# Splitting the column one-hot instruction of an edge placement in two, in a graph network and mixture-of-experts kernel

## The reference

```python
x = x + gnn(layernorm(x), W1, b1, W2, b2, edges=(src, dst))
#   agg  = segment_sum(x[dst], src);  mean = agg / max(count, 1)
#   gnn  = x @ W1.T + b1 + mean @ W2.T + b2
x = x + moe(layernorm(x), Wg, bg, w1, b1, w2, b2)
#   top 2 of 8 experts by score, softmax over the two scores,
#   each expert: relu(x @ w1[e].T + b1[e]) @ w2[e].T + b2[e]
```

## Time and profile before

| | |
|---|---|
| median of 3 runs | 1958.64 us (1956.25 to 1959.66) |
| span of the profiled execution, first to last instruction | 1953.6 us |
| runs' median less that span | 5.0 us |
| PE, PEld, DVE, ACT, POOL busy, share of the span | 90, 76, 50, 57, 61% |
| granted TensorE clock, mean over the span | 0.981 |

### The profile page before, as it was taken

How to read it: one execution, slowest core, us unless ns; L and a number is a source line. 1 busy time by engine, 2 the same in 40 slices (tenths; PEclk the granted TensorE clock), 3 DMA queues, 4 the chain that set the end, 5 groups by cost and what they waited for, 6 DMA issues and landing times.

```text
span 1953.6 us, 41490 instructions
## 1 busy us (share of the span) xinstructions
PE 1762.7 (90%) x11167; PEld 1488.9 (76%) x11167; DVE 967.4 (50%) x2315; ACT 1118.8 (57%) x3316; POOL 1194.5 (61%) x1141
## 2 busy tenths in 40 slices
PE   6888998899887888878887889999999999999997
PEld 4655875588555677656665768999999999999997
DVE  6868977898467887633334786311111111111111
ACT  5964875477544699765652667544444444444443
POOL 1167777778777777777777753454454455444543
PEclk9989999999999999999999999999999999999999
DMA  9323333333333333344543777724424424242421
GB/s 313 102 87 103 94 97 103 103 88 87 100 103 106 100 97 96 100 128 138 143 138 110 236 243 242 216 40 124 127 44 117 102 60 123 38 126 38 124 36 20
DMA packets 113112, 224.31 MB, mean 115 GB/s; under 512 B 27286, under 2 KB 76604, under 8 KB 107094
## 3 DMA queue, kind: packets, MB, share of 16 engines
q0 software_dynamic: 61152, 129.45, 26.6%
q1 hardware_dynamic: 32576, 74.98, 11.3%
q10 hardware_dynamic: 19254, 18.32, 3.0%
HBM read 371.77 MB, written 34.91 MB: 208 GB/s over the span
## 4 chain that ended last, share of the span: by engine, by line
PE 45%; POOL 30%; issue 11%; DMA 6%; DVE 4%; ACT 1%; SPq 1%; DVEq 0%; POOLq 0%; ACTq 0%
POOL arena L650 30%; PE bank L1315 19%; PE bank L1331 18%; DMA arena<-ytab,arena 4%; PE bank L1280 2%; PE bank L1055 2%; PE bank L1303 1%; PE bank L1101 1%; DVE agg L1949 1%; DMA gw<-in_gw2t 1%; SPq L465 1%; DMA ytab<-arena 1%; DMA agg<-in_b 0%; ACT arena L738 0%; ACT arena L753 0%
## 5 line engine op out<-in xcount | busy, mean ns | idle before, releaser
L650 POOL DMA_INDIRECT arena<-ytab,arena x784 | 801.5, 1022 | 240.1 <-issue 228.9
L1280 PE MATMUL bank<-arena 128*128 x2356 | 627.5, 393 | 121.3 <-SPq L525 120.5
L1280 PEld LDWEIGHTS bank<-arena 128*128 128x128 f32 x2356 | 412.4, 195 | 221.4 <-issue 160.7
L948 ACT ACTIVATE arena<-bank,agg 128x128 f32<-128x128 f32 x840 | 308.7, 368 | 400.4 <-PE bank L1315 343.0
L1315 PEld LDWEIGHTS bank<-arena,agg 128*128 128x128 f32 x3360 | 392.2, 192 | 5.6 <-issue 0.7
L1315 PE MATMUL bank<-arena,agg 128*128 128x128 f32 x3360 | 393.8, 276 | 0.3 <-issue 0.3
L1949 DVE TENSOR_TENSOR agg<-agg,bank 128x257 f32 x589 | 247.8, 421 | 292.8 <-PE bank L1280 252.7
L1331 PE MATMUL bank<-agg,arena 128*128 128x256 f32 x1680 | 380.1, 379 | 0.3 <-DMA agg<-in_b 0.3
L683 POOL DMA_INDIRECT out<-arena x105 | 171.0, 1629 | 323.6 <-issue 229.3
L1331 PEld LDWEIGHTS bank<-agg,arena 128*128 128x128 f32 x1680 | 311.0, 190 | 38.5 <-DMA agg<-in_b 0.6
L794 ACT ACTIVATE arena<-lanes,arena 128x128 f16<-128x128 f16 x816 | 247.9, 386 | 21.2 <-DVEq L1577 21.2
(11 more groups left out here) (275 smaller groups left out, 1655.3 us busy)
## 6 DMA issues: line engine op xcount, KB each, us to landing
agg<-in_w SPq DMA_DIRECT2D x210, 1024.0 KB
agg<-in_b SPq DMA_DIRECT2D x105, 128.0 KB
arena<-ytab,arena POOLq DMA_INDIRECT x784
ytab<-arena SPq DMA_DIRECT2D x12, 512.0 KB, 3.2
arena<-in_xt ACTq DMA_DIRECT2D x24, 256.0 KB, 2.9
node<-in_x SPq DMA_DIRECT2D x6, 896.0 KB, 12.3
agg<-in_xt SPq DMA_DIRECT2D x6, 896.0 KB, 12.9
out<-node ACTq DMA_DIRECT2D x6, 896.0 KB
```

What stands on the lines that cost most here:

```text
L650: pool.indirect_dma_start(out=rows[:, v % RU, h, 0:D], out_offset=None, in_=ytab[:, :], in_offset=bass.IndirectOffsetOnAxis(ap=rowidx[g % ...
L948: act.activation(hT[:, m, :], hidden_bank(j, m)[:, 0:T], ACT.Relu, bias=b1b[:, b, m:m + 1]).then_inc(s_fr, 1)
L1280: mm = pe.matmul(bank[bank_of(n)][:, 0:W], onehot[n // QUAD % 2][:, n % QUAD, h, :], pair[:, h * W:(h + 1) * W], start=(h == 0), stop=(h = ...
```

## The change

From the second group on (s = 1, 2, 3) the one instruction that makes the column one-hot of a tile is made as two, for the first four edge columns and for the last four. The second carries the semaphore increment. Both write the same buffer as before, with the same values. For s = 0 the instruction stays whole. Number of tiles that it touches: 22 + 30 + 32 = 84.

```diff
--- before.py
+++ after.py
@@ -1470,8 +1470,14 @@
                 if j % PB == 2:
                     v.wait_ge(s_ohf, OH0[s + 1])
                 v.tensor_tensor(in_pairs(ohq[j % PB][0:EP]), counted(PC, P), pairs(pos_cq[0:EP, 1, c:c + PC, :], PC, P), ALU.is_equal).then_inc(s_q, 1)
-                v.tensor_tensor(in_pairs(ohc[j % PB][0:EP, :, 0:CH[s]]), counted(PC, CH[s]), pairs(pos_cq[0:EP, 0, c:c + PC, :], PC, CH[s]),
-                                ALU.is_equal).then_inc(s_c, 1)
+                if s:
+                    h = PC // 2
+                    v.tensor_tensor(in_pairs(ohc[j % PB][0:EP, 0:h, 0:CH[s]]), counted(h, CH[s]), pairs(pos_cq[0:EP, 0, c:c + h, :], h, CH[s]), ALU.is_equal)
+                    v.tensor_tensor(in_pairs(ohc[j % PB][0:EP, h:PC, 0:CH[s]]), counted(h, CH[s]), pairs(pos_cq[0:EP, 0, c + h:c + PC, :], h, CH[s]),
+                                    ALU.is_equal).then_inc(s_c, 1)
+                else:
+                    v.tensor_tensor(in_pairs(ohc[j % PB][0:EP, :, 0:CH[s]]), counted(PC, CH[s]), pairs(pos_cq[0:EP, 0, c:c + PC, :], PC, CH[s]),
+                                    ALU.is_equal).then_inc(s_c, 1)
                 v.wait_ge(s_q, j + 1)
                 if s == 0:
                     m = PC - BY_ACT
```

## The result

The changed kernel takes 1945.49 us (median of 4 runs, 1942.63 to 1947.36), beside 1959.15 us for the kernel before (4 runs, 1956.25 to 1961.55). The ratio is 0.9934 with a 95% interval of 0.9919 to 0.9950, so the change takes off 13 us, between 10 and 16. Forecast were 1945.6 us and a gain of 13 us.

What follows compares the result with a forecast made beforehand. The prediction took POOL's back-to-back gathers, stretched by DVE instructions, to bound the kernel. From the median of 1958.6 us it took 13 us, the middle of 15.0 and 10.8, giving 1945.6 us, range 1939 to 1953 us.

Steps and rivals of the forecast that it cites:

- POOL sets the pace and the end follows it: The 784 gathers on POOL never wait for the ring; a saving before 1106.85 us moves all that follows.
- A two-input DVE instruction holds a gather until 0.13 us before its end: A gather starting while L1473 runs is held; 45 such gathers were stretched by 27.2 us in all.
- The second half lets the gather in: A waiting gather goes on between L1473's halves; the rival, shut out by the second, meant 1963.3 us, chance 0.05.
- Durations and price on DVE: Halves of L1473 take 0.510, 0.643 and 0.672 us; 84 extra instructions cost 5.9 us of DVE time, hidden beside the gathers.
- The gain, 31.4 - 16.4 or 27.2 - 16.4, middle 13 us: Gather stretch saved on L1473: 15.0 us by rule on both sides, 10.8 us from the observed stretch; 13 us taken.
- if it meets an instruction at a random moment: Stretch rule for gathers every 1.25 us: mean w x w / (2 x 1.25 us) per instruction, w = duration - 0.13 us.
- Nothing else changes: Beyond L1473's hold nothing moves: the semaphore comes 0.07 us later in a tile, and no DMA is added.
- The 5.0 us that the prediction put outside the span: The runs' median lay 5.0 us above the profiled span of 1953.6 us, and was taken as unchanged.
- the phases don't mix: Rival: gathers let go sooner meet the next DVE instruction, giving back 4 us or double; 1952 us, chance 0.07.
- The signs: Expected in the trace: gathers' busy sum about 788 us, last start near 1135 us, stretch falling most beside group 2's placement.
- Held by one instruction only: A stretched gather waits for the end of the DVE instruction it starts in, not for the next one.
- The next list: Rival: group 1's row numbers, ready 6.3 us early, come too late for POOL; half the gain lost, 1952 us, chance 0.07.

Runs made afterwards that it cites:

- 50 whole: Kernel before plus 50 unused two-input DVE instructions of 125 x 2000 f16 beside group 3's gathers; 1984.05 us, ratio 1.0112.
- 50 pairs: Kernel before plus, at 50 places beside group 3's gathers, two unused two-input DVE instructions of 125 x 1000 f16 each; 1972.42 us, ratio 1.0062.
- 50 with one input: Kernel before plus 50 unused DVE reductions over 1024 f16 elements, one SBUF input, beside group 3's gathers; 1961.51 us, ratio 0.9999.
- tiny: Kernel before, L1473 whole, with one 125 x 1 DVE instruction put in front of it in each of the 84 tiles; 1960.43 us, ratio 1.0002.
- the three with 50 additions: Kernel before with 50 whole, 50 pairs or 50 with one input added beside group 3's gathers; 1984.05, 1972.42 and 1961.51 us.
- Six and two: Kernel before with the column one-hot of groups 1 to 3 cut into six edge columns, then two; 1953.37 us, ratio 0.9968.
- quarters: Kernel before with the column one-hot of groups 1 to 3 in four instructions of two edge columns each; 1935.78 us, ratio 0.9878.
- the uneven cuts: Kernel before with the column one-hot of groups 1 to 3 in two uneven pieces, in either order; 1953.37 and 1944.91 us.
- quarters, wide: As quarters, with L1405 also in two and L1661 in two (f16) or four (f32); 1933.52 us, ratio 0.9878 to the kernel before.
- others: Kernel before, L1473 whole, with L1472 and L1486 of groups 1 to 3 each made in two; 1958.06 us, ratio 0.9997.
- tile halves: Changed kernel with L1472 and L1486 of groups 1 to 3 in two as well; 1947.45 us, ratio 0.9939 to the kernel before.
- eighths: Kernel before with the column one-hot of groups 1 to 3 in eight instructions, one per edge column; 1982.96 us, ratio 1.0116.
- all split: As tile halves, with L1405 of groups 1 to 3 in two and L1661 in two (f16) or four (f32); 1939.09 us, ratio 0.9894.
- two and six: Kernel before with the column one-hot of groups 1 to 3 cut into two edge columns, then six; 1944.91 us, ratio 0.9933.

## Why the prediction was right, point by point

- **POOL sets the pace and the end follows it.** Right. Fourteen kernels with the last gather from 1122.6 to 1177.6 us end 805 to 810 us later.
- **A two-input DVE instruction holds a gather until 0.13 us before its end.** Right, and shown apart: 22.3 us for 50 whole, 11.2 us for 50 pairs, 1.1 us for 50 with one input.
- **The second half lets the gather in.** Right for halves, where it was given 0.05 against. It fails for most gathers that start in pieces of 172 to 250 elements, and now and then for others: twice in tiny, with L1473 whole.
- **Durations and price on DVE.** L1475 and L1476 take 0.51, 0.64 and 0.67 us as forecast (0.68 in one group). The price of the instruction is hidden; tiny showed it.
- **The gain, 31.4 - 16.4 or 27.2 - 16.4, middle 13 us.** The net was met, 12.9 us by the ratio, but out of two errors that cancel, so that the number is in part luck. First, 27.2 instead of 31.4 is habit and not chance: the four other kernels that keep L1473 whole and in its place (the three with 50 additions, and tiny) have 30.7, 27.5, 27.6 and 26.3 us of hold by it. Secondly, the halves hold for 8.6 us, not 16.4. So L1473's part of the gain is 27.2 - 8.6 = 18.6 us, over the 15.0 that the sum had as its upper end. The term that failed is "if it meets an instruction at a random moment". L1473 stands behind L1472. A start that falls into L1472 is moved to that one's end, and the next comes 1.25 us after it, beyond the pair. Only starts in the first 0.65 us behind L1472 are free to happen. With the same lengths w that gives 27.7 us whole and 10.8 us halved. The starts bear it out: in the kernel before and the three with 50 additions, 186 gathers start within a whole L1473, all in its first 0.61 us, although it lasts up to 1.2 us. In tiny, 46 start in the first 0.60 us and 16 at 1.14 to 1.15 us, where the hold is over. Six and two bear it out in who is hit, not in how much time the order costs.
- **Nothing else changes.** Wrong by some 5 us, the 18.6 less the 12.9. A gather let go sooner starts its successor sooner, and what ends at L1486 (now L1492) rose from 5.2 to 7.8 us, at L1661 from 8.9 to 10.1 us. How much each takes is not shown by one trace: in the five kernels with L1473 whole in its place L1486 has 4.6 to 9.2 us, in quarters 7.6, and in the uneven cuts 10.7 and 12.7. L1405 rose from 2.8 to 6.1 us, but in the four kernels with L1473 whole it has 6.1, 4.6, 7.8 and 5.0 us, so there the kernel before's own trace was low. That is also why the two profiles differ by 10.4 us in the gathers' busy time and the medians by more. The 5.0 us that the prediction put outside the span were too many: the changed kernel's profiled execution took 1946.23 us at a span of 1944.1, 2.1 us outside. The profiled execution of before was thus near 1955.7 us, below its fastest timed run, and the gain had to be taken from the medians, as it was. This is the rival "the phases don't mix" in a small measure; it ate 5 us, not 8.
- **The signs.** The busy sum came to 791.1 us where about 788 were named, and the last gather starts 2.4 us later than the 1135 named. Stretch was to fall most beside group 2's placement, but fell by 3.5 us there and beside group 1's, and by 7.1 us beside group 3's.
- **Held by one instruction only.** Not so for all gathers of the kernel before: its longest, 2.41 us from 136.11 us on, and one of 2.40 us are held over L1416 and L1417 together, as is the gather from 136.37 us on above. The prediction took them for part of the rest that the change leaves as it is, which is right for the sum.
- **The next list.** Not reached by the change: the list was ready at 274.12 us and wanted at 276.50 us, 2.4 us later instead of 6.3. It was the right place to look: quarters, wide ran into it, and into the ring.

The profile of the changed kernel at the end of group 1's list (L1550, the old L1544), and the first gather of that group:

```profile
273.87 0.25 DVE L1550 TENSOR_SCALAR arena<-arena 128x172 int32<-128x172 int32 x1
276.50 0.95 POOL L650 DMA_INDIRECT arena<-ytab,arena  x1 [0.30 <-issue]
```

## What stays open

Why a gather that starts 0.19 to 0.21 us into an instruction is sometimes shut out over all that follow without a pause, and why it happens to most that start in pieces of 172 to 250 elements, no run here tells. In others and in tile halves 12 of the 13 start at that offset. Of the 28 shut out in all kernels but eighths, 17 do; six start 0.02 to 0.04 us into an instruction, three (in all split) at 0.46 to 0.47 us, one each at 0.09 and 0.28 us. Of gathers at the same offset some are let go. The offset may point to a race at the moment at which the gather asks, but it was not varied by itself. With pieces of 344 to 500 elements one gather is shut out in quarters and four in quarters, wide; between these and 250 elements the limit lies, and what sets it is open too. Open as well is why the copy L1417 and the cast L1454, with one input, hold a gather and the reductions don't.

## What to carry to other kernels

Where GpSimd issues indirect DMAs back to back and they are the pace, look for gathers longer than the median and set their ends against VectorE's. What costs is not VectorE's busy share but the length of each of its instructions with two inputs from SBUF (and of some copies and casts with one, so go by the ends of the gathers): cutting the longest in two or four pays as long as something else hides the extra instructions, and it stops paying when pieces get so short that a waiting gather no longer gets in between them. Reckon the meeting of two periodic queues from the order of the instructions, not from random moments, and expect part of what is freed to be caught again by the next instruction.

## What the runs showed that was not expected

That eight pieces hold gathers longer than one: 63 gathers shut out, with 50.8 us of stretch, and a kernel 1.16% slower than before, where two and four pieces made it 0.66% and 1.22% faster. And that the same cut, six and two or two and six, gives 6 or 13 us by its order alone. And that in every trace three gathers beside L1417, a copy with one input from SBUF, end only 0.12 to 0.13 us after it, the two longest of the kernel before among them.
